# Expert down projection: one 512-column product per load, and the output split between ScalarE and VectorE

## The reference, cut to what matters

```python
router_probs = softmax(flat_x @ router_w)
topk_w, topk_idx = top_k(router_probs, 2)
topk_w = topk_w / sum(topk_w)
for e in range(8):
    h = gelu(flat_x @ w_fc[e])                      # 256 -> 1024
    out = out + combine[:, e:e + 1] * (h @ w_proj[e])   # 1024 -> 256
```

## Time and profile before

| | us |
|---|---|
| median of three runs | 781.47 |
| lowest, highest run | 780.15, 792.13 |
| span of the profiled execution | 780.3 |

### The profile page before, as it was taken

One profiled execution on the slowest core, in us unless ns is written; L12 is line 12 of the kernel. 1 busy time (PEld: TensorE's weight loads), 2 busy tenths in 40 slices (PEclk: granted clock), 3 DMA queues, 4 the chain that ended last, 5 costly groups with the idle time before them and its releaser, 6 DMA issues. The chain is left out here.

```text
span 780.3 us, 16994 instructions
## 1 busy us (share of the span) xinstructions
PE 666.8 (85%) x5010; PEld 630.4 (81%) x5010; DVE 578.8 (74%) x1249; ACT 398.4 (51%) x671; POOL 456.9 (59%) x371
## 2 busy tenths in 40 slices
PE   1588998888860799999999999999999999999993
PEld 0476887777750699989898989898989898989893
DVE  8765687777765678787878787878787878787862
ACT  2703544445431565656465646565656565656551
POOL 5002236676546457676767666767576767676764
PEclk9998999999965699999999999999999999999997
DMA  9706722222223555432122222122222132213222
GB/s 343 229 0 228 279 102 83 70 81 81 78 78 117 152 148 138 104 89 48 31 51 34 48 32 50 29 53 32 50 32 50 29 53 32 50 29 53 33 37 27
DMA packets 39480, 64.06 MB, mean 82 GB/s; under 512 B 3808, under 2 KB 34848, under 8 KB 38304
## 3 DMA queue, kind: packets, MB, share of 16 engines
q0 software_dynamic: 14304, 18.92, 14.1%
q1 hardware_dynamic: 14816, 34.55, 12.8%
q10 hardware_dynamic: 10336, 10.31, 5.2%
HBM read 37.96 MB, written 25.81 MB: 82 GB/s over the span
## 5 line engine op out<-in xcount | busy, mean ns | idle before, releaser
L599 POOL TENSOR_TENSOR pj_lo<-w_ffn,pj_hi 128x1024 fp32r<-128x1024 f32 x78 | 194.3, 2492 | 130.8 <-ACT pj_hi L640 123.9
L1204 DVE TENSOR_TENSOR fc_lo<-w_ffn,fc_hi 128x1024 fp32r<-128x1024 f32 x78 | 111.6, 1470 | 85.3 <-ACT fc_hi L640 85.3
L589 POOL DMA_INDIRECT out<-y,add_id x78 | 126.0, 1615 | 45.2 <-issue 43.8
L1204 DVE TENSOR_TENSOR h_lo<-h,h_hi 128x512 fp32r<-128x512 f32 x156 | 143.4, 919 | 5.4
L1220 DVE CAST h_hi<-h 128x512 fp32r<-128x512 f32 x156 | 118.1, 757 | 5.7 <-ACT h L763 5.7
L1500 PE MATMUL psP<-pj_hi,h_hi 128*128 128x256 f32 x312 | 94.3, 302 | 27.1 <-DVE h_lo L1204 27.1
L640 ACT ACTIVATE pj_hi<-w_ffn 128x1024 fp32r x78 | 82.8, 1061 | 67.5 <-PE psO L1500 64.3
L640 ACT ACTIVATE fc_hi<-w_ffn 128x1024 fp32r x78 | 78.3, 1052 | 31.3 <-issue 27.7
L1500 PEld LDWEIGHTS psP<-pj_hi,h_hi 128*128 128x128 f32 x312 | 59.9, 192 | 36.5 <-DVE h_lo L1204 35.0
L1500 PE MATMUL psO<-pj_lo,h_hi 128*128 128x256 f32 x312 | 88.7, 284 | 0.0
L1500 PE MATMUL psO<-pj_hi,h_lo 128*128 128x256 f32 x312 | 88.6, 284 | 0.0
(11 more groups left out here) (249 smaller groups left out, 1623.2 us busy)
## 6 DMA issues: line engine op xcount, KB each, us to landing
w_ffn<-in_w_ffn SPq DMA_DIRECT2D x8, 2048.0 KB, 7.8
xg<-slots ACTq DMA_DIRECT2D x38, 265.0 KB, 3.3
xc<-in_x_ch SPq DMA_DIRECT2D x4, 1024.0 KB, 8.5
out<-x SPq DMA_DIRECT2D x16, 256.0 KB, 2.1
x<-in_x_tok SPq DMA_DIRECT2D x1, 3072.0 KB, 24.3
slots<-fill SPq DMA_DIRECT2D x9, 265.0 KB, 4.7
out<-y,add_id POOLq DMA_INDIRECT x78, 4.0
w_in<-in_w_in SPq DMA_DIRECT2D x1, 1024.0 KB, 13.3
```

Of the source, the lines that this page charges most:

```text
L589: nc.gpsimd.indirect_dma_start(out_d, bass.IndirectOffsetOnAxis(ap=add_id[:, s:s + 1], axis=0), y[:, s, :], None, compute_op=ALU.add).then ...
L599: nc.gpsimd.tensor_tensor(pj_lo[:, 4 * a:4 * a + 4, :], w_ffn[:, bass.ds(e, 1), (2 + a) * DFF:(3 + a) * DFF].rearrange("p a (c d) -> p (a ...
L1204: v.tensor_tensor(out, whole, upper.bitcast(F32), ALU.subtract).then_inc(done, 1)
```

## The change

- `pj_hi` and `pj_lo` become the two halves of one tile `pj` of [P, FC, 2, D]: chunk f holds 256 upper and, next to them, 256 lower columns.
- `down(g)`: for each chunk and token tile one product of h_hi with all 512 columns of `pj` into the whole bank (left half upper, right half lower), and one of h_lo with the upper 256 into the left half. There are two loads and two products where there were three. The sum of the left and the right half is no longer made in PSUM.
- ScalarE's `outputs` becomes `outputs_rest`, at the same place: y = right half x weight, with a new semaphore `y_rest_ready`.
- VectorE gets `outputs`: y = left half x weight + y, and that raises `y_ready`. It stands behind `hidden(g, 1)`.

```diff
-        pj_hi, pj_lo = (ff(n, [P, FC, D], F32R) for n in ("pj_hi", "pj_lo"))
+        pj = ff("pj", [P, FC, 2, D], F32R)
+        pj_hi, pj_lo = pj[:, :, 0, :], pj[:, :, 1, :]
...
-            def outputs(g):
+            def outputs_rest(g):
                 act.wait_ge(down_mm, g * 2 + 2)
                 if later(g):
                     act.wait_ge(y_added, g * 32)
                 for s, bank in enumerate((psP, psO)):
-                    nc.scalar.activation(y[:, s, :], bank[:, 0:D], ACT.Copy,
-                                         scale=slot_w[:, bass.ds(g, 1), s]).then_inc(y_ready, 1)
+                    nc.scalar.activation(y[:, s, :], bank[:, D:2 * D], ACT.Copy,
+                                         scale=slot_w[:, bass.ds(g, 1), s]).then_inc(y_rest_ready, 1)
...
                 if g_on(g - 1):
-                    outputs(g - 1)
+                    outputs_rest(g - 1)
...
+            def outputs(g):
+
+                for s, bank in enumerate((psP, psO)):
+                    dve.wait_ge(y_rest_ready, g * 2 + s + 1)
+                    v.scalar_tensor_tensor(y[:, s, :], bank[:, 0:D], slot_w[:, bass.ds(g, 1), s], y[:, s, :],
+                                           ALU.mult, ALU.add).then_inc(y_ready, 1)
+
             def dve_group(g, par):
                 if g_on(g + 1):
                     fc_lower(g + 1, 1 - par, expert_of(g + 1))
                 hidden(g, 0)
                 hidden(g, 1)
+                if g_on(g - 1):
+                    outputs(g - 1)
                 if g_on(g + 1):
                     slot_meta(g + 1)
...
                     for s, bank in enumerate((psP, psO)):
-                        for n, (w, m) in enumerate(three(h_hi, h_lo, pj_hi, pj_lo)):
-                            ins = mm(bank[:, 0:D], w[:, f, s * P:(s + 1) * P], m[:, f, :],
-                                     start=(f == 0 and n == 0), stop=(f == FC - 1 and n == 2))
+                        tok = slice(s * P, (s + 1) * P)
+                        mm(bank[:, :], h_hi[:, f, tok], pj[:, f, :, :].rearrange("p n d -> p (n d)"),
+                           start=(f == 0), stop=False)
+                        ins = mm(bank[:, 0:D], h_lo[:, f, tok], pj_hi[:, f, :], start=False, stop=(f == FC - 1))
```

More of the change, by code:

```diff
@@ L329, in hybrid_block @@
         ld_w = sem("ld_w")
-        xg_loaded, xg_t_mm, x_hi_ready, x_lo_ready, meta_read, up_mm, gelu_done, h_hi_ready, h_ready = (
-            sem(n) for n in ("xg_loaded", "xg_t_mm", "x_hi_ready", "x_lo_ready", "meta_read", "up_mm", "gelu_done", "h_hi_ready", "h_ready"))
+        xg_loaded, xg_t_mm, y_rest_ready, x_hi_ready, x_lo_ready, meta_read, up_mm, gelu_done, h_hi_ready, h_ready = (
+            sem(n) for n in ("xg_loaded", "xg_t_mm", "y_rest_ready", "x_hi_ready", "x_lo_ready", "meta_read", "up_mm", "gelu_done", "h_hi_ready", "h_ready"))
         fc_hi_ready, fc_lo_ready, pj_hi_ready, pj_lo_ready, down_mm, y_ready, id_ready, y_added = (
@@ L808, in _ @@
             run_groups(act, act_group)
-            outputs(GROUPS - 1)
+            outputs_rest(GROUPS - 1)
         @block.vector
@@ L1252, in _ @@
             run_groups(dve, dve_group)
+            outputs(GROUPS - 1)
         @block.tensor
```

## The result

The changed kernel takes 856.5 us (median of four runs, 855.6 to 857.5) against 782.4 us: a ratio of 1.095, 95% interval 1.093 to 1.098. It is slower by 74 us; the forecast was 845, slower by 64. The profiled execution has a span of 854.7 us.

A forecast was written before the change was run, and what follows sets the result against it. The loop through ScalarE, GpSimd's second pj_lo and VectorE's first h_lo was taken to bound the kernel at 13.01 us; 14.51 + 0.2 = 14.7, 1.7 more, times 38 is 64.6, so 780.3 becomes 845 us, range 824 to 870.

The forecast's parts named there:

- The cause: Down projection: y_ready now comes from VectorE after both h pairs and two additions, so TensorE may start 1.95 us later.
- A group at full clock: Expert stage: the new loop from y_ready through GpSimd and VectorE closes at 14.51 us instead of 13.01.
- Which loop: Expert stage: scatter-adds, pj_lo and fc_lo end at 9.29, just behind 9.2 when GpSimd's second pj_lo wants to start.
- only the wait: Rival: second pj_lo meets no fc_lo, clock stays up; path TensorE, Gelu, pj_lo, VectorE; 825 to 835 us, chance 0.15.
- buys nothing: Down projection: TensorE is on the loop at only one point with 0.1 us to spare, so its saved 0.21 us gains nothing.
- TensorE's term: Down projection: 16 loads fewer per group, 512-column step 0.227 us, saving 0.21 us per group, ends 0 and 0.43.
- The fall of the clock: TensorE: a 2.5 us wait brings half clock, group 14.9 us, 0.4 more; counted in half the groups, 0.2 us.
- The rival with the clock in every group: Expert stage: clock falls in every group, with slower GpSimd subtractions 15.3 us a group, 867 us; chance 0.17.
- The order that turns: Rival: VectorE gets both h pairs in ahead of GpSimd's second pj_lo, TensorE's 11.9 us bounds; 738 us, chance 0.04.

The follow-up runs named there:

- e2: Kernel before, with y_ready given by two one-column copies on VectorE behind the second h pair; output and products as before: 815.4 us, ratio 1.042.
- e9: Changed kernel with slot_meta ahead of VectorE's additions: 912.6 us, ratio 1.165 to the kernel before.
- e6: Changed kernel, VectorE order fc_lo half, first h pair, additions, second h pair, other fc_lo half; ScalarE's right half ahead of its second Gelu: 772.4 us.
- e3: Kernel before, with two additions of unused result on VectorE behind the second h pair, ahead of slot_meta; y_ready stays with ScalarE: 831.7 us, ratio 1.062.
- e1: Changed kernel with only its products: ScalarE reads the left half and gives y_ready, VectorE adds nothing: 781.7 us, ratio 0.999 to the kernel before.
- e5: Changed kernel, ScalarE's right half ahead of its second Gelu, VectorE's additions between upper and lower copy of the first h pair: 797.9 us, ratio 1.020.
- e7: Kernel before, without additions, VectorE order fc_lo half, first and second h pair, other fc_lo half: 772.4 us, ratio 0.986.
- e10: e6 with ScalarE's load of the next group's rows moved from ahead of pj_hi to behind fc_hi: 773.8 us, ratio 0.988 to the kernel before.
- e11: e7 with ScalarE's load of the next group's rows moved from ahead of pj_hi to behind fc_hi: 772.9 us, ratio 0.987 to the kernel before.
- e12: e10 with the second fc_lo half moved to the end of VectorE's group, behind x_lo: 796.5 us, ratio 1.018 to the kernel before.

## Why the prediction was right, and where its sizes were off

- **The cause.** Right: the giver of y_ready. e2 has it alone at 33 us; e9 makes it later by 0.8 us and the groups at full clock longer by 0.7; e6 takes the additions out of the way and the loss is gone.
- **What the additions push back besides.** The prediction has no term for slot_meta. By e3 its lateness with y_ready left alone costs 49 us, nearly the 55 that the changed kernel loses at full clock: giving y_ready back to ScalarE would hardly have been enough, though this was not tried in the changed kernel. That the sum came out without this term is luck; y_ready ends last by about 1 us at pj, and so the other delay doesn't show.
- **A group at full clock.** Forecast 14.51, measured 14.41. Two errors of the working cancel, which is luck. The working counts from y_ready, here 599.70. GpSimd's second subtraction started at 9.6 (609.30), not 9.2, and ended at 12.0 (611.70), not 11.55: TensorE took 0.22 us to start, not 0.06, and 5.65 for the down projection, not 5.55, and from the Gelu to the subtraction it was 2.03, not 1.91. Behind it VectorE needed 2.4 us to y_ready (611.70 to 614.10), not 2.96, since h_hi had gone ahead of the subtraction and only h_lo was left.
- **Which loop.** I had GpSimd's scatter and fc_lo end last, by 0.1 us over the path through TensorE and the Gelu. It is the other: the subtraction of 609.30 waited for pj_hi, 2.47 us, and fc_lo was done at 609.06. So the path is that of the rival "only the wait", and TensorE's saved 0.2 us a group is on it; "buys nothing" holds for the kernel before (e1), not for this one, where it was not tried apart.
- **TensorE's term.** Right. Taken 0.227 us for 512 columns and 0.21 saved per group, measured 0.23 to 0.24 with 0.11 to 0.12 for the 256 columns behind, and 0.2 saved (5.89 to 5.69). The trace doesn't tell whether the 13 ns each belong to the 16 loads or to the 16 products that are gone.
- **The fall of the clock: the term that was mis-sized.** "14.9, 0.4 more than without the fall", in half of the groups. Measured 1.4 more (15.82 against 14.43 on the mean), in 14 of 36. In the group from 628.74 the down projection took 7.25 us instead of 5.65, 1.6 against my 1.4. GpSimd's subtraction started 1.63 later and lasted 0.2 longer, since VectorE's h_lo was in hand (639.75 to 642.35). What I had counted on was that the first h pair would get ahead of it and save 1.0; it did get ahead (639.40), but saved 0.6 only, as h_hi had been ahead in the short groups as well. 1.63 + 0.20 - 0.61 = 1.22, this group's excess. Over the 14 groups the excess is 1.4. In all: 14.97 instead of 14.7, times 38, is 10 us; the profiled span, 854.7, lies 9.7 above the forecast, and the median of the runs another 1.8.
- **The rival with the clock in every group** is what e9 shows, where the wait is 3.1 us. **The order that turns** is what e5's short groups and e6 show; in the changed kernel itself it did not turn.
- **From e2 to the changed kernel.** e2 takes 13.84 us a group, the changed kernel at full clock 14.41, 0.57 more. From the end of GpSimd's second subtraction to the start it is 2.63 us in the changed kernel (611.70 to 614.33) and 1.96 in e2 (627.50 to 629.46): the two additions with what stands around them lie 0.66 us longer between the second pair and the start than e2's two copies (1.01 against 0.35). The subtraction ends 0.1 us earlier behind the start of the down projection (11.78 against 11.88): that is what is left there of TensorE's saving. Together they give the 0.57.
- **What stays open.** In the changed kernel itself neither of the two delays, of y_ready and of slot_meta, was cured alone; what each is worth is known from e2 and e3 only, which start from the kernel before.

## What to carry to other kernels

When work moves from one engine to another, look first at the semaphore that it gives: what stands ahead of it in the new engine's queue, and who waits. The same two additions cost nothing behind slot_meta, 49 us ahead of it, and nothing beside GpSimd's subtraction. In the changed kernel they pushed back two things at once, and only the later one showed, so look for the second before curing the first. A load saved on an engine that waits anyway bought nothing in three comparisons (e1; e6 with e7; e10 with e11). And count a longer wait of TensorE twice: once for itself, and once for the clock that may fall behind it.

## What I had not expected of the hardware

- How steeply the falls come with the wait: none with 1.64 us in every group (e2), 14 of 36 with 2.3 us (85.8 us in 37 waits), 28 of 35 with 3.1 us (e9). Each fall halved the clock for some 3.4 us, by the windows of 628 to 634, and cost 1.4 us on the mean in the changed kernel (15.82 against 14.43 a group) and 1.5 in e9 (16.69 against 15.17). Filling 1.95 us of the wait with products that nobody reads took the falls away.
- VectorE's scalar_tensor_tensor with one operand in PSUM is not held up by GpSimd's subtraction (0.48 us at 611.77, in e6, inside 611.45 to 614.08), while a copy or subtraction of 512 elements within SBUF waits for its end (2.62 and 2.82 us instead of 0.42 and 0.69).
- GpSimd's issue of the first scatter-add of a group took 1.66 us in the kernel before, 2.0 in the changed one and 2.65 in e6 and e10, where it lies beside VectorE's second fc_lo half. e12 differs from e10 only in the place of that half, and there it takes 1.56, so it is that half which lengthens it by 1.1 us; what makes it 2.0 in the changed kernel was not tried. In e6, and in e12:

```profile
602.50 2.65 POOL L590 DMA_INDIRECT out<-y,add_id  x1 [0.79 <-issue]
```

```profile
564.29 1.56 POOL L590 DMA_INDIRECT out<-y,add_id  x1 [0.79 <-issue]
```
